# A head's maximum with the mask added by VectorE, four jobs in eight with their counts as logarithms, and guard keys made by ScalarE

## What is computed

```python
lam = LAMBDA_MAX * exp(-ALPHA * u_prev); use_sparse = lam >= 1.0
s_scores = einsum('bhsd,bhskd->bhsk', Q, Kg) * 0.25          # Kg = K[:, :, idx]
s_scores = where(prior_index_mask, s_scores, -inf)
sparse_out = einsum('bhsk,bhskd->bhsd', softmax(s_scores, -1), Vg)
x = x + L0_ffn(L0_cond(x)); x = x + L1_ffn(L1_cond(x))        # outer form of the whole
```

## Time and profile before

| | |
|---|---|
| median of 3 runs | 569.64 us |
| the profiled execution: its own time | 570.82 us |
| its span, first to last instruction | 568.4 us |
| TensorE busy | 521.5 us (92%) |
| VectorE busy | 408.6 us (72%) |
| ScalarE busy | 225.7 us (40%) |
| GpSimd busy | 84.2 us (15%) |

### The profile page before, as it was taken

One profiled execution on the slowest core, in us unless ns is written; L12 is line 12 of the kernel. 1 busy time (PEld: TensorE's weight loads), 2 busy tenths in 40 slices (PEclk: granted clock), 3 DMA queues, 4 the chain that ended last, 5 costly groups with the idle time before them and its releaser, 6 DMA issues.

```text
span 568.4 us, 7403 instructions
## 1 busy us (share of the span) xinstructions
PE 521.5 (92%) x2649; PEld 360.3 (63%) x2649; DVE 408.6 (72%) x788; ACT 225.7 (40%) x381; POOL 84.2 (15%) x94
## 2 busy tenths in 40 slices
PE   3897888999899999889969999999999999999896
PEld 1454445454454445436748887888878888788775
DVE  4887879878887777845867598483884839847295
ACT  4204476667665656764526240042400415003100
POOL 3002544315133120300141000010000100000000
PEclk9999699999999999999999999999999999999999
DMA  7200011101010000000451000100001000010000
GB/s 250 57 2 0 1 37 38 37 2 38 1 39 1 1 0 2 1 1 0 114 146 38 1 1 20 46 10 0 2 18 47 11 2 0 20 46 2 9 12 31
DMA packets 11756, 15.37 MB, mean 27 GB/s; under 512 B 5954, under 2 KB 8258, under 8 KB 11714
## 3 DMA queue, kind: packets, MB, share of 16 engines
q1 hardware_dynamic: 11714, 14.83, 8.5%
HBM read 12.73 MB, written 2.10 MB: 26 GB/s over the span
## 4 chain that ended last, share of the span: by engine, by line
PE 39%; DVE 6%; POOL 2%; issue 1%; DMA 1%; ACT 1%; SPq 0%; DVEq 0%; POOLq 0%
PE psG L1546 4%; PE psG L1545 4%; PE psG L1544 4%; PE psM L1544 3%; PE psM L1545 3%; PE psM L1546 3%; PE psS L1544 3%; PE psS L1545 3%; PE psS L1546 3%; PE psO L1544 3%; PE psO L1546 3%; PE psO L1545 3%; DVE hT_lo L1694 1%; DVE hT_hi L1692 1%; DMA staged<-ew_dram 1%
## 5 line engine op out<-in xcount | busy, mean ns | idle before, releaser
L737 DVE TENSOR_REDUCE few_Qa<-psG 128x2 fp32r<-128x512 f32 x116 | 74.7, 686 | 28.5 <-PE psG L506 28.4
L657 ACT ACTIVATE Pr<-psS 128x512 f32<-128x512 f32 x128 | 71.4, 599 | 28.5 <-PE psS L528 19.5
L744 DVE SCALAR_TENSOR_TENSOR Pr<-Pr,few_W 128x1024 f32<-128x1024 f32 x48 | 72.8, 1520 | 10.2 <-ACT Pr L657 10.1
L524 PE MATMUL psS<-few_QAT,few_KP 128*128 128x512 f32 x128 | 52.9, 457 | 10.5 <-ACT Pr L657 9.8
L504 PE MATMUL psG<-few_KG,QG 128*128 128x512 f32 x116 | 53.0, 515 | 2.9 <-DVE few_Qa L737 2.9
L1655 ACT ACTIVATE V<-psS,cols 128x512 f32<-128x512 f32 x16 | 11.0, 690 | 103.3 <-PE psS L1546 102.6
L1694 DVE TENSOR_TENSOR hT_lo<-V,hT_hi 128x512 fp32r<-128x512 f32 x64 | 46.5, 726 | 2.2
L506 PE MATMUL psG<-Mneg,few_identb 128*128 128x512 bf16 x116 | 46.8, 403 | 0.0
L524 PEld LDWEIGHTS psS<-few_QAT,few_KP 128*128 128x128 f32 x128 | 22.3, 188 | 38.2 <-issue 30.7
L1692 DVE CAST hT_hi<-V 128x512 fp32r<-128x512 f32 x64 | 34.2, 535 | 12.7 <-ACT V L1655 6.2
L540 PE MATMUL psO<-Pr,few_VA 128*17 128x512 f32 x256 | 33.5, 598 | 0.0
(11 more groups left out here) (251 smaller groups left out, 1194.7 us busy)
## 6 DMA issues: line engine op xcount, KB each, us to landing
Pr<-xT_dram SPq DMA_DIRECT2D x2, 1024.0 KB, 8.6
staged<-w_dram SPq DMA_DIRECT2D x4, 512.0 KB, 3.7
x1T<-xT_dram SPq DMA_DIRECT2D x4, 512.0 KB, 4.2
staged<-ew_dram SPq DMA_DIRECT2D x4, 512.0 KB, 4.0
out_dram<-y SPq DMA_DIRECT2D x16, 128.0 KB, 1.7
staged<-fc_dram SPq DMA_DIRECT2D x2, 512.0 KB, 3.8
Pr<-wqkv_dram SPq DMA_DIRECT2D x1, 768.0 KB, 4.9
staged<-fc2a_dram SPq DMA_DIRECT2D x1, 512.0 KB, 3.4
```

The lines of the kernel that those rows point to most:

```text
L524: mm = nc.tensor.matmul(psS[:, f, :], self.KP[:, u % 2, j, r * P:r * P + P], self.QAT[:, u % 2, j // 2, q], start=True, stop=not logged)
L657: nc.scalar.activation(Pr[:, i % JOBS, 512 * f:512 * f + 512], psS[:, f, :], ACT.Exp, scale=SCALE).then_inc(self.s["s_exp"], 1)
L737: nc.vector.tensor_reduce(self.Qa[:, f % SLOTS, st, 2 * p:2 * p + 2, 48], self.guard_bank(i)[0][:, p, :].rearrange("p (h t) -> p h t", h=2 ...
L744: nc.vector.scalar_tensor_tensor(pr, pr, FMAX, self.W[:, r, :], ALU.min, ALU.mult).then_inc(self.s["s_prob"], 1)
```

## The change

The second matmul of a guard job goes, and with it TensorE's wait for `Mneg`. VectorE's reduction over two heads is replaced by one `tensor_tensor_reduce` per head, which adds `Mneg` to the scores, scales by -1, writes the result back over the scores in PSUM and keeps the minimum. VectorE now waits once for `Mneg` itself. `LOGGED` goes from jobs 3 and 7 of each eight to 1, 3, 5 and 7, so 16 more of the 64 score jobs have four more matmuls and no `weigh`. The guard keys are made by ScalarE with four activations of 128x256, one per head, in place of one GpSimd instruction.

```diff
-LOGGED = (3, 7)
+LOGGED = (1, 3, 5, 7)
@@ pool
-                    if what == "guard_keys":
-                        pool.wait_ge(self.s["kt_out"], i // 2 + 1)
-                        if i >= 2:
-                            pool.wait_ge(self.s["g_scores"], 2 * JOBS * (i - 1))
-                        hm = headmask[:, HG * (i % 2):HG * (i % 2) + HG]
-                        nc.gpsimd.tensor_tensor(
-                            self.KG[:, i % 2, :, :],
-                            self.KT[:, None, :].to_broadcast([P, HG, FEW_KEYS]),
-                            hm[:, :, None].to_broadcast([P, HG, FEW_KEYS]), ALU.mult).then_inc(self.s["kg_ready"], 1)
@@ tensor, guard
-                        pe.wait_ge(self.s["neg_out"], min(2, st // HALF + 1 + 2 * (u > 0)))
...
-                            nc.tensor.matmul(o, QG[:, (u // 2) % 2, st * P:st * P + P],
-                                             self.KG[:, u % 2, 2 * p:2 * p + 2, :], start=True, stop=False)
-                            mm = nc.tensor.matmul(o, self.identb[:, :],
-                                                  Mneg[:, None, st * FEW_KEYS:(st + 1) * FEW_KEYS].to_broadcast([P, 2, FEW_KEYS]),
-                                                  start=False, stop=True)
+                            mm = nc.tensor.matmul(o, QG[:, (u // 2) % 2, st * P:st * P + P],
+                                                  self.KG[:, u % 2, 2 * p:2 * p + 2, :], start=True, stop=True)
@@ act
+                    if what == "guard_keys":
+                        act.wait_ge(self.s["kt_out"], i // 2 + 1)
+                        if i >= 2:
+                            act.wait_ge(self.s["g_scores"], 2 * JOBS * (i - 1))
+                        for h in range(HG):
+                            mm = nc.scalar.activation(self.KG[:, i % 2, h, :], self.KT[:, :], ACT.Copy,
+                                                      scale=headmask[:, HG * (i % 2) + h:HG * (i % 2) + h + 1])
+                        mm.then_inc(self.s["kg_ready"], 1)
@@ vector, guard
+                            dve.wait_ge(self.s["neg_out"], 2)
+                        tile = i % JOBS
                         for p in range(2):
                             dve.wait_ge(self.s["g_scores"], 2 * i + p + 1)
-                            nc.vector.tensor_reduce(self.Qa[:, f % SLOTS, st, 2 * p:2 * p + 2, 48],
-                                                    self.guard_bank(i)[0][:, p, :].rearrange("p (h t) -> p h t", h=2), AX.X,
-                                                    ALU.max, negate=True).then_inc(self.s["g_max"], 1)
+                            for h in range(2):
+                                seen = self.guard_bank(i)[0][:, p, h * FEW_KEYS:(h + 1) * FEW_KEYS]
+                                mm = nc.vector.tensor_tensor_reduce(
+                                    seen, seen,
+                                    Mneg[:, tile * FEW_KEYS:(tile + 1) * FEW_KEYS], -1.0, FMAX, ALU.add, ALU.min,
+                                    self.Qa[:, f % SLOTS, st, 2 * p + h, 48:49])
+                            mm.then_inc(self.s["g_max"], 1)
```

## The result

The changed kernel takes 572.46 us (median of 6 runs) beside 569.78 for the kernel before in the same runs: a ratio of 1.005 with a 95% interval of 1.0037 to 1.0064. The change made it slower by half a per cent, about 2.7 us, where 4 us less were forecast. Its profiled execution took 572.95 us with a span of 571.1.

What follows compares the result with a forecast made beforehand. VectorE was taken to bound the first guard jobs and to wait for TensorE in the middle, with neither alone setting the end's pace. Terms +1.3, +2.4, -9.4 and +1.5 gave -4.2 us, hence 565.4 us, range 560 to 579.

Steps and rivals of the forecast that it cites:

- the middle's term: From the first exponential to the last guard job, 52 steps: TensorE's lighter work was to save 9.4 us.
- ScalarE's insertions and all coupling: In the middle: 2.0 us allowed for engines waiting on each other and ScalarE's seven later sets of key activations.
- the -11.4 of the count: TensorE's matmuls in the middle: 23.9 us of masks removed, 12.5 of logging added, net 11.4 us less.
- VectorE's sum: VectorE's work in the middle: 22.9 us more, 14.8 and some 7 less, about +1 us.
- The pair: VectorE's two guard instructions per head: a slot of 0.41 us, bounds 0.40 to 0.68; a guard job 1.64 instead of 1.20.
- The twelve guard jobs: First guard jobs, before the score jobs: VectorE the bound throughout, 19.7 us in place of 16.7.
- The credit of 0.6 us: Between VectorE's first twelve guard jobs and the first exponential: 1.8 us in place of 2.44, by earlier transposes.
- The opening: Before the first guard reduction: ScalarE's four activations ahead of the count casts were to add 1.3 us.
- the end: The last twelve score jobs: three more logged jobs were to add 1.5 us, between 0.6 and 2.9.
- Rival 2: Middle gains little because TensorE waits for late exponentials or VectorE: no change, sum -0.5 us, 569; chance 0.13.
- Rival 1: VectorE becomes the bound with a pair at 0.50 us: slower, sum +9.5 us, 579; chance 0.33.
- the three signs of being wrong: A pair above 0.46 us, TensorE waiting for VectorE's maxima in the middle, or a granted clock under 1.00 there.

Runs made afterwards that it cites:

- b2: The kernel before with logged jobs 1, 3, 5 and 7 of each eight and nothing else changed: 571.58 us, ratio 1.0035.
- a3: The changed kernel with guard keys on GpSimd and logged jobs 3 and 7 as before, leaving only the mask on VectorE: 564.11 us, ratio 0.9904.
- a1: The changed kernel with the guard keys made by GpSimd again, all else of the change kept: 565.48 us, ratio 0.9935.
- b1: The changed kernel with ScalarE's guard keys of units 1 to 7 placed one at a time behind the exponentials of four steps: 567.21 us, ratio 0.9960.
- a4: The kernel before with the guard keys moved from GpSimd to ScalarE, nothing else: 573.76 us, ratio 1.0078.
- a2: The changed kernel with only jobs 3 and 7 logged, as before; mask on VectorE and keys on ScalarE kept: 571.69 us, ratio 1.0042.
- c1: a1 with the first 12 guard jobs' masks on TensorE and only jobs 3 and 7 logged in the last 12 score jobs: 560.34 us, ratio 0.9852.
- c2: c1 with no logged job at all among the last 12 score jobs: 560.99 us, ratio 0.9829.
- b4: a1 with the order of before in guard jobs 0 to 11, where TensorE adds the mask: 564.82 us, ratio 0.9918.

## Why the prediction was wrong, step by step

- **What bounds the middle.** "So in the middle VectorE waits for TensorE" was a right reading and a wrong conclusion. VectorE's wait doubled in b2 for 1.3 us, and moving 23.9 us of matmuls from TensorE to VectorE in a3 gave 6.0 (154.0 to 148.0), with VectorE then busy 138.5 of 148.0 us and the clock lower for a while. No engine is full in the kernel before: TensorE has 12 us free, VectorE 27, ScalarE 54. The pace would then come from the order: a score matmul waits for the exponential of the job before, which waits for the score matmul of that job, and the guard jobs have such a loop with VectorE. That is argued from the waits; no run takes the loops apart.
- **The step that failed** is the middle's term, and in it this sentence: "most lies in its idle time, and I put what is left into the coupling below". I gave ScalarE's insertions and all coupling 2.0 us together. The insertions alone cost 5.6 us in the middle (151.6 with them, 146.0 in a1). b1 shows that it is their place: the same activations one at a time cost 0.4. ScalarE does have idle time, but it does not lie where they stand: of the five sets of keys in that stretch four cost 1.6 to 1.7 us each, all of the 1.6 that they take, the first cost 0.1, and 1.2 us came back later. The measured -2.4 is the -11.4 of the count, plus 5.6 for the keys, plus 3.4 that remain for all other coupling.
- **The rest of the middle.** Without the keys it gained 8.0 us (a1) where the matmul count gave 11.4, a coupling of 3.4 against my 2.0. Size, not sign. The mask gave 6.0 of it and logging 2.0 (148.0 to 146.0), though a3's 148.0 has a lowered clock in it. Logging gave back 0.5 at the end there (30.2 to 30.7), 1.4 with the mask on TensorE and 2.0 with ScalarE's keys. VectorE's work was mis-sized too, the other way: not about 1 us more but 13 less (127.2 to 113.8 busy), from the cheaper pair and from nearly all of the stretching gone, 13.7 us and not 6 to 8. So VectorE's sum was no reason for the small gain.
- **The pair.** 0.38 against 0.41, just under my lower end of 0.40. The twelve guard jobs came to 18.3 in place of 19.7 us.
- **The credit of 0.6 us** before the first exponential did not come, 2.7 us passed from VectorE's end to it, against 2.4 before. Unit 2's keys stand there too, ahead of the table load; with GpSimd's keys it is 2.1 (a1: 20.4 us to the exponential, 18.3 of them guard jobs).
- **The opening** was 1.6 to 1.9 in place of 1.3, **the end** 1.2 against 1.5.
- **Rivals.** Rival 2 had the mechanism word for word, "exponentials that come late behind the new activations", at a chance of 0.13 and with "ScalarE has 54 us free in the middle" against it; that free time was no argument. It put the middle at -5.7 and the sum at -0.5; the middle's -2.4 is nearly all of the way from there to +2.7. Rival 1's pair price never came near.
- **Range and signs.** 572.46 us lies between 560 and 579 by luck: the range went past 568 for rival 1 alone, whose price of 0.50 did not come. And none of the three signs of being wrong showed. The pair was under 0.46, TensorE's guard matmuls waited 0.6 us for VectorE in the middle, and the clock was 1.00 in the middle. I had named no sign for a late exponential.

The keys cost 3.6 us in the middle with the mask on TensorE (a4) and 7.2 with it on VectorE and two logged jobs (a2 against a3). Lined up by score jobs, the difference stands where one of the two clocks is low: a2 falls behind by 1.5 us at jobs 18 to 20, 2.7 at 26 to 28 and 1.3 at 34 to 35, in the rows of 0.83, 0.70 and 0.83 above, and a3 by 1.8 at job 7, in its row of 0.66. Without these 3.7 some 3.5 are left, as in a4. Whether the stops before the exponentials bring the falls about was not tried apart and stays open.

## What to carry to other kernels

An engine's free time says nothing on whether an instruction can be added to it; where in the queue it stands does, and ahead of the one instruction that two engines pass back and forth it cost its full length here in four places of five, of which a fifth came back later. Before pricing a removal by an engine's work, ask whether any engine is full: here 24 us of TensorE's work, moved to VectorE, were worth 6, and 12 more, with weighing passes saved for them, cost 1.3. And split a change of three parts before judging it: one part here was worth 1%, one cost 0.8% alone and more with the first, and the third was small, so that the whole looked like a small loss.

## What the runs showed of the hardware

- An instruction on VectorE that keeps a minimum and its accumulator read of 128x1 (rows of 455 and 139 ns) together take a slot of 0.382 us: the next head's instruction starts with the read, and the read adds only 0.04 us to the 0.34 of the main instruction.
- Writing the sum back into the PSUM bank that it is read from costs nothing to be seen: the first row is 0.42 us long with the next start after 0.34, as the 128x256 instruction of the earlier trace rows that reads PSUM and writes elsewhere. The 256 rows lie between 418 and 468 ns, and none was stretched, while a weighing pass in the same trace reached 1955 ns.
- An activation with a per-partition scale takes a slot of 0.40 us for 128x256, a cast of the same size 0.30.
- TensorE's granted clock was 0.81 in the first guard jobs before and 0.77 after. In a3, a4 and a2 it rose to 1.00 and fell again in the middle (rows of 0.66 and 0.70). The same program took 146.1 us at 1.00 throughout (c1) and 147.6 with a row of 0.83 (c2, b4).
- A weighing pass on VectorE of 1.2 us took 3.18 us beside a 128x1024 instruction of 2.40 on GpSimd.
